# First layer of a two-layer graph network: who issues the zeros, where the first norms are taken, and the order of norm and one-hot

## The chip, the cores and the metric

The kernel runs on one core of one Trainium2 chip. The metric is device time in microseconds for one launch; the time given for a kernel is the median of its runs. All times inside a profile are microseconds from the start of the span, on one profiled execution.

## What is computed

A graph has 12,500 nodes with 256 features each and 200,000 edges (`src`, `dst`, a weight). Cut to what matters:

```
h = relu(layernorm(x))                 # per node, over 256 features
x = x + segment_sum(w[:,None] * (h @ weight)[dst], src)      # layer 0
h = relu(layernorm(x))
x = x + attention over the edges(h) @ Wo.T + bo              # layer 1, 8 heads
```

In layer 0 the edge's message is read at `dst` and summed at `src`. The edges come sorted by `dst`. The change is in layer 0 alone.

## The kernel before, in words

**Layer 0** first builds tables and then runs one long loop. The 200,000 edges are cut into T = 1563 tiles of 128 edges. Since `dst` is sorted, the edges of one tile read few blocks of 128 nodes; each (tile, block) pair is a *row* j, of which there are J = 1660. The loop takes them in NW = 208 windows of W = 8 rows.

For each row, a one-hot of the `dst` within its block (VectorE, `Oh`, line 852) and a weighted matrix that says which edges of the tile have the same `src` (ScalarE, `same`, lines 765 to 776) are multiplied on TensorE (718), copied to SBUF by ScalarE (799) and multiplied with the normed features `h` (734). VectorE adds the product to the tile's slot of `mtw` (`add`, 825) twelve rows behind the window (LAG). A finished tile is added by GpSimd with one indirect DMA of 128 rows into one of four copies of the output in DRAM, `sums[t % 4]` (701). SyncE stands between: it counts finished rows into tiles (`a_tile`), which GpSimd waits for, and landed tiles (`a_landed`), which VectorE waits for before it uses one of 16 slots again.

**The four copies must be zero** before anything is added to them. 72 DMAs write zeros, 704 KB each, 18 for each copy (`zeros`, line 168; `zeroed.per` is 18). All are issued by ScalarE: `sums[0]` and `sums[1]` in the tables' block (36), `sums[2]` and `sums[3]` at the head of the loop's block (36). GpSimd waits for the 18 of `sums[t]` before tile t, for t = 0 to 3 (line 697).

**The norms.** `h` holds all 98 blocks of 128 nodes; they are normed in 14 groups of 7 blocks. Group n needs its rows of `x` (`x_rows`, one DMA of 896 KB, line 162), 7 times two VectorE instructions (836, 838), one square root on ScalarE (442), two small VectorE instructions (434, 436) and 7 ScalarE activations (745). TensorE waits for enough of them (`a_h`).

**The stages.** Every `Block` is a stage: each engine runs its part in the written order, and the next stage begins when all engines have ended. The stages around the change:

- The tables (block with lines 482 to 632). SyncE writes three fields of the edges to DRAM (487 to 491), copies one of them as `srows` (492) and then issues `x_rows` 0 to 2. GpSimd gathers 13 pieces of the fields (508), four in flight; TensorE transposes each (534) and VectorE copies them out (616) with a count (609) before each piece. ScalarE only issues 36 zeros.
- The loop (lines 672 to 887). SyncE issues `x_rows` 3 to 5 and `edge_rows` 0 to 2 (512 KB each, line 669), then begins its counting. ScalarE issues its 36 zeros, then does its part of norms 0 and 1, then `same(0)`, `same(1)`, then the loop over g, two to a window; later `x_rows` and `edge_rows` are issued from there. VectorE does its part of norms 0 and 1, then the windows: in window w norm w + 2 comes first, then `Oh`, then for 8 rows the compare (862) and `add`, then places (868 to 880).

The two sides of a norm wait for each other within one call, on VectorE in `norm_dve`:

```python
e.wait_ge(S(name + "_root"), n)      # ScalarE's square root of this group
e.reciprocal(sc[:, 1, b], sc[:, 0, b]).then_inc(S(name + "_norm"), 1)
```

After layer 0 the engines meet, the four copies are added up, and layer 1 runs; it is the same in both kernels.

Of the kernel before, what the change touches and what calls it, by code (L numbers as in the profile page):

```python
# [7 lines left out]
P = 128  # L8
# [4 lines left out]
NB = 98  # L13
# [9 lines left out]
NS = 4  # L23
ZW = 11 * P
G = 7
# [65 lines left out]
def build(nc, x, src, dst, edge_weight, weight, Wq, bq, Wk, bk, Wv, bv, Wo, bo, out):  # L91
# [17 lines left out]
    with ExitStack() as top:  # L109
# [52 lines left out]
            e.dma_start(h[:, b0:b1, :], x[b0 * P:b1 * P, :].rearrange("(b p) d -> p b d", p=P)).then_inc(  # L162
                xin.sem(g), 16)

        def zeros(e, k):
            part = sums[k].rearrange("(p r) d -> p (r d)", p=P)
            for i in range(zeroed.per):
                e.dma_start(part[:, i * ZW:(i + 1) * ZW], zero[:, :]).then_inc(zeroed.sem(k * zeroed.per + i), 16)

        def edge_loads(e, vec, to, sem):  # L170
            full = 12 * P * P
# [282 lines left out]
        wT = sb(l0a, "wT", [P, JP])  # L454
        sT = sb(l0a, "sT", [P, JP])
        rf = sb(l0a, "rf", [P, 1])
        with ExitStack() as stack:
            NF = 4
            blk = sb(stack, "blk", [P, 13], I32)
            cvec = sb(stack, "cvec", [P, 13])  # L460
            df = sb(stack, "dstf", [P, 13, P])
# [21 lines left out]
            @block.sync  # L483
            def _(e):
                table = fields.rearrange("(c p) f -> p c f", p=P)
                e.wait_ge(edges[2].sem(2), edges[2].value(2))
                e.dma_start(table[:, :, 2 * P:3 * P], wf[:, :, :]).then_inc(rows.sem(0), 16)
                e.wait_ge(S("pr_fields"), 1)
                e.dma_start(table[:, :, P:2 * P], df[:, :, :]).then_inc(rows.sem(1), 16)
                e.wait_ge(S("pr_fields"), 2)  # L490
                e.dma_start(table[:, :, 0:P], sf[:, :, :]).then_inc(rows.sem(2), 16)
                e.dma_start(srows.rearrange("a (c p f) -> p (a c) f", p=P, f=P), sf[:, :, :]).then_inc(put.sem(0), 16)
                for g in range(3):
                    x_rows(e, g)
                e.wait_ge(put.sem(0), put.value(0))

            @block.gpsimd
# [38 lines left out]

            @block.scalar
            def _(e):
                for k in range(NS // 2):
                    zeros(e, k)  # L540

            @block.vector
            def _(e):
                e.wait_ge(edges[1].sem(2), edges[1].value(2))
                e.tensor_scalar(blk[:, :], ints[:, 1, :, 0], 7, None, ALU.logical_shift_right).then_inc(
                    S("pr_blk"), 1)
# [64 lines left out]

                for c in range(13):
                    count(c)
                    for i, to in enumerate((dloc, sT, wT)):
                        e.wait_ge(S("pr_turn"), 3 * c + i + 1)
                        e.tensor_copy(to[:, c * P:(c + 1) * P], psum[3 * (c % 2) + i][:, 0:P]).then_inc(
                            S("pr_column"), 1)
# [22 lines left out]

        with ExitStack() as stack:
            LAG, BACK = 12, 5
            epst = sb(stack, "epst", [P, 1])
            stt = sb(stack, "stt", [P, 4, 6])
            mv = sb(stack, "mv", [P, NB, 2])
            sc = sb(stack, "sc", [P, 3, NB])
            Oh = sb(stack, "Oh0", [P, 2, W, P])
            Sr = ints[:, :, :, :].rearrange("p a b c -> p (a b c)").bitcast(F32)[:, 0:3 * W * P].rearrange(
                "p (s j e) -> p s j e", s=3, j=W)
# [22 lines left out]
            @block.sync  # L672
            def _(e):
                (e_reg[e.engine], *_) = registers(e, "l0s")
                regs = registers(e, "l0t")
                e.sem_inc(S("a_landed"), 1)
                for w in range(3):
                    x_rows(e, w + 3)
                    edge_rows(e, w)
                for t in range(T + BACK):  # L680
                    if t < T:
                        if t % 4 == 0:
                            e.load(regs[:4], lastrow[0:1, t:t + 4])
                            last = [e.snap(r, min_val=1, max_val=J) for r in regs[:4]]

                        e.wait_ge(S("a_row"), last[t % 4])
                        e.sem_inc(S("a_tile"), 1)
                    if t >= BACK:
                        e.wait_ge(sent.sem(t - BACK), sent.value(t - BACK))
                        e.sem_inc(S("a_landed"), 1)  # L690
# [47 lines left out]

            @block.scalar
            def _(e):  # L740
                def norm(n):
                    norm_act(e, "a", n, n + 1, mv, sc, epst)
                    e.wait_ge(S("a_norm"), 2 * n + 2)
                    for b in range(n * G, n * G + G):
                        e.activation(h[:, b, :], h[:, b, :], ACT.Relu, bias=sc[:, 2, b:b + 1],
                                     scale=sc[:, 1, b:b + 1]).then_inc(S("a_h"), 1)

                for k in range(NS // 2, NS):
                    zeros(e, k)
                norm(0)  # L750
                norm(1)
                (e_reg[e.engine], *_) = registers(e, "l0c")
                regs = registers(e, "l0h")

# [27 lines left out]
                for g in range(J // 4):  # L782
                    same(g + 2)
                    v = g // 2
                    if g % 2 == 0:
                        if v + 2 < NG7:
                            norm(v + 2)
                        if v + 6 < NG7:
                            x_rows(e, v + 6)
                        if v + 6 == NG7 - 1:  # L790
                            e.dma_start(h[0:NLAST, NB - 1, :], x[(NB - 1) * P:N, :]).then_inc(hw[24].sem, 16)
                        if v and v + 2 < NW:
                            e.wait_ge(S("a_more"), v * W)
                            e.wait_ge(S("a_off"), v * W)
                            edge_rows(e, v + 2)
# [7 lines left out]
            def _(e):  # L803
# [22 lines left out]
                                           in1=psum[2 + j // 2 % 4][:, j % 2 * D:j % 2 * D + D], op0=ALU.mult,  # L826
                                           op1=ALU.add).then_inc(S("a_row"), 1)

                def norm(n):
                    e.wait_ge(xin.sem(n), xin.value(n))  # L830
                    if n == NG7 - 1:
                        e.wait_ge(hw[24].sem, 16)
                    for b in range(n * G, n * G + G):
                        if b >= 4:
                            e.wait_ge(S("a_stat"), 2 * b - 6)
                        e.bn_stats(stt[:, b % 4, :], h[:, b, :]).then_inc(S("a_stat"), 1)
                        e.wait_ge(S("a_stat"), 2 * b + 1)
                        e.bn_aggr(mv[:, b, :], stt[:, b % 4, :]).then_inc(S("a_stat"), 1)
                    norm_dve(e, "a", n, n + 1, mv, sc)

                e.memset(epst[:, :], 1e-5)
                e.memset(one[:, :], 1.0).then_inc(S("a_one"), 1)
                norm(0)
                norm(1)
                for w in range(NW):
                    j0 = w * W
                    n = min(W, J - j0)
                    if w + 2 < NG7:
                        norm(w + 2)
                    if w >= 2:  # L850
                        e.wait_ge(S("a_weights"), 2 * w - 2)
                    e.tensor_tensor(Oh[:, w % 2, 0:n, :], bcast(iota[:, :], n), rows_of(dloc[:, j0:j0 + n]),  # L852
                                    ALU.is_equal).then_inc(S("a_oh"), 1)
                    e.wait_ge(came.sem(w), came.value(w))
                    for j in range(j0, j0 + n):
                        if j % 4 == 0:
                            e.load(regs[:4], toff[0:1, j:j + 4])
                            row = [e.snap(r, min_val=0, max_val=W - 1) for r in regs[:4]]
# [1149 lines left out]
```

## Time and profile before

| what | us |
|---|---|
| median of 3 runs | 6892.29 (6885.31 to 6894.68) |
| the profiled execution's own time | 6941.69 |
| its span | 6939.9 |
| granted TensorE clock, mean | 0.796 |
| busy: PE / PE loads / DVE / ACT / POOL | 4544.0 / 2978.0 / 4539.5 / 3970.3 / 4648.7 |
| first and last indirect add of layer 0 (line 701) | 233.9 / 3231.6 |

PE is TensorE's matmul, PEld its weight load, DVE VectorE, ACT ScalarE, POOL GpSimd, SPq and ACTq the DMA issues of SyncE and ScalarE. Busy time says how long an engine had an instruction; what an engine waited for stands behind it in brackets (`[idle before <-releaser]`). "issue" is time for which the profile shows no wait. The granted clock is given as a share of 2.4 GHz.

### The profile page before, as it was taken

What the parts mean: (1) busy time and instruction counts of PE and PEld (TensorE: products, weight loads), DVE (VectorE), ACT (ScalarE), POOL (GpSimd) and SP (SyncE); (2) the same over time, 40 slices, a digit from 0 to 9 for tenths busy, and PEclk for the clock granted to TensorE, in tenths of its full rate; (3) what the DMA queues carried; (4) which work ended last, traced back from release to release, by engine and by line L of the source; (5) the groups of instructions that cost most, each with busy time, mean ns of one, the idle gap of its engine ahead of it and who ended that gap; (6) DMA issues with size and microseconds to landing.
All of it is one profiled execution on the core that took longest, in us unless ns stands there. A gap on an engine that the chain in (4) does not pass through costs nothing. (4 is left out here: it accounts for less than half of the span.)

```text
span 6939.9 us, 112013 instructions
## 1 busy us (share of the span) xinstructions
PE 4544.0 (65%) x19717; PEld 2978.0 (43%) x16197; DVE 4539.5 (65%) x12295; ACT 3970.3 (57%) x14482; POOL 4648.7 (67%) x3716
## 2 busy tenths in 40 slices
PE   1356666666666666664886677777777777777777
PEld 1244444444444545553553333334333333434335
DVE  4565555555555666663554777777777777777766
ACT  0665555555555555552332577777777767777761
POOL 1478888888888888887554566666666666666630
PEclk6677777777777777776998888888888888888889
DMA  8767777777777777777874566666666666676756
GB/s 303 196 103 107 106 106 105 104 107 106 108 107 106 106 110 108 109 109 167 274 260 136 173 188 192 192 190 195 194 192 195 200 200 197 201 206 201 204 151 194
DMA packets 644159, 1129.71 MB, mean 163 GB/s; under 512 B 74529, under 2 KB 466795, under 8 KB 643445
## 3 DMA queue, kind: packets, MB, share of 16 engines
q0 software_dynamic: 367600, 678.97, 50.2%
q1 hardware_dynamic: 223985, 273.78, 12.1%
q10 hardware_dynamic: 51860, 169.74, 7.3%
q14 instruction: 546, 4.47, 0.2%
q8 instruction: 168, 2.75, 0.2%
HBM read 929.80 MB, written 451.51 MB: 199 GB/s over the span
## 5 line engine op out<-in xcount | busy, mean ns | idle before, releaser
L701 POOL DMA_INDIRECT sums<-mtw,posIw x1563 | 2492.0, 1594 | 599.5 <-issue 404.5
L1249 POOL DMA_INDIRECT kv<-kvt,sI x1760 | 1774.2, 1008 | 1027.4 <-ACT room L1631 596.1
L1631 ACT ACTIVATE room<-kv,pp 128x33 f32<-128x33 f32 x8800 | 1932.3, 308 | 107.2 <-issue 101.8
L734 PE MATMUL ps<-h,wf 128*128 x3320 | 1220.8, 522 | 310.0 <-DVE mtw L825 237.3
L1551 PE MATMUL ps<-room,Of 128*128 128x264 f32 x3520 | 1130.8, 459 | 372.2 <-DVE acc L1734 189.0
L718 PE MATMUL ps<-Mw,Oh 128*128 128x128 f32 x3320 | 672.6, 368 | 918.6 <-DVE Oh L852 918.6
L825 DVE SCALAR_TENSOR_TENSOR mtw<-mtw,cont,ps 128x256 f32 x1660 | 794.1, 478 | 620.2 <-SPq L690 459.9
L718 PEld LDWEIGHTS ps<-Mw,Oh 128*128 128x128 f32 x3320 | 631.7, 274 | 1035.3 <-DVE Oh L852 1004.4
L734 PEld LDWEIGHTS ps<-h,wf 128*128 128x128 f32 x3320 | 816.9, 263 | 590.1 <-issue 451.4
L1551 PEld LDWEIGHTS ps<-room,Of 128*128 128x128 f32 x3520 | 707.6, 219 | 659.6 <-issue 278.6
L799 ACT COPY wf<-ps 128x512 f32<-128x512 f32 x415 | 242.4, 584 | 1234.4 <-PE ps L718 902.9
L1496 PE MATMUL ps<-qb,OT 128*128 x3520 | 699.3, 301 | 0.0
L1530 PE MATMUL ps<-qb,OT 128*128 x1760 | 534.0, 303 | 244.6 <-DMA qb<-qt 189.0
L862 DVE SCALAR_TENSOR_TENSOR junk<-ints,sT,tri 128x128 f32<-128x128 f32 x1660 | 574.7, 347 | 87.8 <-issue 87.4
L880 DVE TENSOR_TENSOR posIw<-sT,step 128x1 f32 x1660 | 265.1, 160 | 473.1 <-DVE step L870 163.4
L1688 DVE TENSOR_TENSOR room<-ps,kv 128x1024 f32<-128x1024 f32 x440 | 532.1, 1209 | 19.9 <-remote 14.3
L1734 DVE SCALAR_TENSOR_TENSOR acc<-acc,keep,ps 128x264 f32 x880 | 422.3, 480 | 184.2 <-remote 113.4
L765 ACT ACTIVATE off<-ints,sT 128x128 f32 x1660 | 530.1, 390 | 19.9 <-issue 8.6
L776 ACT ACTIVATE Mw<-off,wT 128x128 f32<-128x128 f32 x1660 | 530.0, 390 | 13.4
L1697 DVE TENSOR_REDUCE room<-room 128x32 f32<-128x1024 f32 x440 | 533.7, 1213 | 0.3
L1530 PEld LDWEIGHTS ps<-qb,OT 128*128 128x128 bf16 x1760 | 189.3, 108 | 701.0 <-issue 641.3
L770 ACT ACTIVATE off<-off,one 128x512 f32<-128x512 f32 x415 | 299.4, 721 | 13.5
(224 smaller groups left out, 4796.5 us busy)
## 6 DMA issues: line engine op xcount, KB each, us to landing
qb<-qt SPq DMA_DIRECT2D x880, 192.0 KB
accd<-acc SPq DMA_DIRECT2D x880, 132.0 KB
ints<-srows ACTq DMA_DIRECT2D x205, 512.0 KB
OT<-drows SPq DMA_DIRECT2D x110, 512.0 KB
sums<-zero ACTq DMA_DIRECT2D x72, 704.0 KB
part<-sums SPq DMA_DIRECT2D x56, 896.0 KB
kv<-kvt,sI POOLq DMA_INDIRECT x1760
kvt<-kvo SPq DMA_DIRECT2D x98, 260.0 KB
```

What stands on the lines that cost most here:

```text
L701: e.indirect_dma_start(sums[t % NS], bass.IndirectOffsetOnAxis(ap=posI[:, t % NP:t % NP + 1], axis=0), mt[:, t % NM, :], None, compute_op= ...
L718: m = e.matmul(psum[g % 2][:, j % 4 * P:j % 4 * P + P], lhsT=Oh[:, j // W % 2, j % W, :], rhs=Mw[:, j % 16, :], start=True, stop=True)
L734: m = e.matmul(psum[2 + q % 4][:, j % 2 * D:j % 2 * D + D], lhsT=BT[:, g % 3, j % 4, :], rhs=h[:, bass.ds(own[j % 4], 1), :].rearrange("p ...
L825: e.scalar_tensor_tensor(out=to, in0=to, scalar=cont[:, j:j + 1], in1=psum[2 + j // 2 % 4][:, j % 2 * D:j % 2 * D + D], op0=ALU.mult, op1= ...
L862: e.scalar_tensor_tensor(out=junk[:, j % 4, :], in0=srow, scalar=sT[:, j:j + 1], in1=tri[:, :], op0=ALU.is_equal, op1=ALU.mult, accum_out= ...
L1249: e.indirect_dma_start(kv[:, s % NK, :], None, kvt, bass.IndirectOffsetOnAxis(ap=sI[:, s:s + 1], axis=0)).then_inc(kvs.sem(s), 16)
L1496: return e.add_instruction(mybir.InstMatmult(name=nc.get_next_instruction_name(), engine=e.engine, start_tensor_calc=False, stop_tensor_ca ...
L1530: e.matmul(to, lhsT=hot, rhs=third(j, 0), start=True, stop=False)
L1551: m = e.matmul(psum[6 + j % 2][:, 0:NH * 33], lhsT=Of[:, w % 2, k % W2, :], rhs=pv[:, k % NV, :], start=(k % 2 == 0), stop=(k % 2 == 1))
L1631: e.activation(pv[:, s % NV, h * 33:h * 33 + 33], kv[:, s % NK, D + h * 33:D + h * 33 + 33], ACT.Copy, scale=pp[:, w % 2, h, s % W2:s % W2 ...
L1688: e.tensor_tensor(prod[:, Q % 2, :, :], banks[:, Q % 2 * 2:Q % 2 * 2 + 2, :].rearrange("p b (a d) -> p (b a) d", d=D), kv[:, s:s + 4, 0:D] ...
L1697: e.tensor_reduce(sims[:, w % 2, :, Q % 4 * 4:Q % 4 * 4 + 4].rearrange("p h i -> p i h"), prod[:, Q % 2, :, :].rearrange("p a (h d) -> p a ...
```

## The change

- `zeros` takes a range of the 72 pieces in place of a copy's number. ScalarE issues pieces 0 to 35 and 36 to 55 in the tables' stage. SyncE issues 56 to 71 at the head of the loop's stage, between its rows of edges and of `x`.
- Norms 0 and 1 are taken in the tables' stage: ScalarE between its two runs of zeros, VectorE after its first count. SyncE issues `x_rows` 0 and 1 before the copy to `srows`. The small tiles of the norm move to the outer scope.
- At the head of the loop's stage only norm 2 is taken. In window w, VectorE makes `Oh` first, then takes the statistics of group w + 3, and ends that norm (`norm_dve`) ahead of the window's fifth row. ScalarE ends group v + 2 (`normed0`) and then takes the root of group v + 3.
- `norm` falls apart into `stats0` and `normed0`, which are shown in the diff.

```diff
--- before.py
+++ after.py
@@ -162,10 +162,11 @@
             e.dma_start(h[:, b0:b1, :], x[b0 * P:b1 * P, :].rearrange("(b p) d -> p b d", p=P)).then_inc(
                 xin.sem(g), 16)
 
-        def zeros(e, k):
-            part = sums[k].rearrange("(p r) d -> p (r d)", p=P)
-            for i in range(zeroed.per):
-                e.dma_start(part[:, i * ZW:(i + 1) * ZW], zero[:, :]).then_inc(zeroed.sem(k * zeroed.per + i), 16)
+        def zeros(e, first, end):
+            for i in range(first, end):
+                at = i % zeroed.per * ZW
+                e.dma_start(sums[i // zeroed.per].rearrange("(p r) d -> p (r d)", p=P)[:, at:at + ZW],
+                            zero[:, :]).then_inc(zeroed.sem(i), 16)
 
         def edge_loads(e, vec, to, sem):
             full = 12 * P * P
@@ -454,8 +455,30 @@
         wT = sb(l0a, "wT", [P, JP])
         sT = sb(l0a, "sT", [P, JP])
         rf = sb(l0a, "rf", [P, 1])
+        epst = sb(l0a, "epst", [P, 1])
+        stt = sb(l0a, "stt", [P, 4, 6])
+        mv = sb(l0a, "mv", [P, NB, 2])
+        sc = sb(l0a, "sc", [P, 3, NB])
+
+        def stats0(e, n):
+            e.wait_ge(xin.sem(n), xin.value(n))
+            if n == NG7 - 1:
+                e.wait_ge(hw[24].sem, 16)
+            for b in range(n * G, n * G + G):
+                if b >= 4:
+                    e.wait_ge(S("a_stat"), 2 * b - 6)
+                e.bn_stats(stt[:, b % 4, :], h[:, b, :]).then_inc(S("a_stat"), 1)
+                e.wait_ge(S("a_stat"), 2 * b + 1)
+                e.bn_aggr(mv[:, b, :], stt[:, b % 4, :]).then_inc(S("a_stat"), 1)
+
+        def normed0(e, n):
+            e.wait_ge(S("a_norm"), 2 * n + 2)
+            for b in range(n * G, n * G + G):
+                e.activation(h[:, b, :], h[:, b, :], ACT.Relu, bias=sc[:, 2, b:b + 1],
+                             scale=sc[:, 1, b:b + 1]).then_inc(S("a_h"), 1)
+
         with ExitStack() as stack:
-            NF = 4
+            NF, ZA, ZB = 4, 36, 56
             blk = sb(stack, "blk", [P, 13], I32)
             cvec = sb(stack, "cvec", [P, 13])
             df = sb(stack, "dstf", [P, 13, P])
@@ -489,9 +512,10 @@
                 e.dma_start(table[:, :, P:2 * P], df[:, :, :]).then_inc(rows.sem(1), 16)
                 e.wait_ge(S("pr_fields"), 2)
                 e.dma_start(table[:, :, 0:P], sf[:, :, :]).then_inc(rows.sem(2), 16)
+                x_rows(e, 0)
+                x_rows(e, 1)
                 e.dma_start(srows.rearrange("a (c p f) -> p (a c) f", p=P, f=P), sf[:, :, :]).then_inc(put.sem(0), 16)
-                for g in range(3):
-                    x_rows(e, g)
+                x_rows(e, 2)
                 e.wait_ge(put.sem(0), put.value(0))
 
             @block.gpsimd
@@ -536,11 +560,15 @@
 
             @block.scalar
             def _(e):
-                for k in range(NS // 2):
-                    zeros(e, k)
+                zeros(e, 0, ZA)
+                for n in range(2):
+                    norm_act(e, "a", n, n + 1, mv, sc, epst)
+                    normed0(e, n)
+                zeros(e, ZA, ZB)
 
             @block.vector
             def _(e):
+                e.memset(epst[:, :], 1e-5)
                 e.wait_ge(edges[1].sem(2), edges[1].value(2))
                 e.tensor_scalar(blk[:, :], ints[:, 1, :, 0], 7, None, ALU.logical_shift_right).then_inc(
                     S("pr_blk"), 1)
@@ -611,6 +639,10 @@
 
                 for c in range(13):
                     count(c)
+                    if c == 0:
+                        for n in range(2):
+                            stats0(e, n)
+                            norm_dve(e, "a", n, n + 1, mv, sc)
                     for i, to in enumerate((dloc, sT, wT)):
                         e.wait_ge(S("pr_turn"), 3 * c + i + 1)
                         e.tensor_copy(to[:, c * P:(c + 1) * P], psum[3 * (c % 2) + i][:, 0:P]).then_inc(
@@ -640,10 +672,6 @@
 
         with ExitStack() as stack:
             LAG, BACK = 12, 5
-            epst = sb(stack, "epst", [P, 1])
-            stt = sb(stack, "stt", [P, 4, 6])
-            mv = sb(stack, "mv", [P, NB, 2])
-            sc = sb(stack, "sc", [P, 3, NB])
             Oh = sb(stack, "Oh0", [P, 2, W, P])
             Sr = ints[:, :, :, :].rearrange("p a b c -> p (a b c)").bitcast(F32)[:, 0:3 * W * P].rearrange(
                 "p (s j e) -> p s j e", s=3, j=W)
@@ -674,9 +702,15 @@
                 (e_reg[e.engine], *_) = registers(e, "l0s")
                 regs = registers(e, "l0t")
                 e.sem_inc(S("a_landed"), 1)
-                for w in range(3):
-                    x_rows(e, w + 3)
-                    edge_rows(e, w)
+                edge_rows(e, 0)
+                x_rows(e, 3)
+                zeros(e, ZB, ZB + 5)
+                edge_rows(e, 1)
+                x_rows(e, 4)
+                zeros(e, ZB + 5, ZB + 10)
+                edge_rows(e, 2)
+                x_rows(e, 5)
+                zeros(e, ZB + 10, NS * zeroed.per)
                 for t in range(T + BACK):
                     if t < T:
                         if t % 4 == 0:
@@ -738,17 +772,8 @@
 
             @block.scalar
             def _(e):
-                def norm(n):
-                    norm_act(e, "a", n, n + 1, mv, sc, epst)
-                    e.wait_ge(S("a_norm"), 2 * n + 2)
-                    for b in range(n * G, n * G + G):
-                        e.activation(h[:, b, :], h[:, b, :], ACT.Relu, bias=sc[:, 2, b:b + 1],
-                                     scale=sc[:, 1, b:b + 1]).then_inc(S("a_h"), 1)
-
-                for k in range(NS // 2, NS):
-                    zeros(e, k)
-                norm(0)
-                norm(1)
+                norm_act(e, "a", 2, 3, mv, sc, epst)
+                normed0(e, 2)
                 (e_reg[e.engine], *_) = registers(e, "l0c")
                 regs = registers(e, "l0h")
 
@@ -783,8 +808,10 @@
                     same(g + 2)
                     v = g // 2
                     if g % 2 == 0:
-                        if v + 2 < NG7:
-                            norm(v + 2)
+                        if 3 <= v + 2 < NG7:
+                            normed0(e, v + 2)
+                        if v + 3 < NG7:
+                            norm_act(e, "a", v + 3, v + 4, mv, sc, epst)
                         if v + 6 < NG7:
                             x_rows(e, v + 6)
                         if v + 6 == NG7 - 1:
@@ -826,33 +853,22 @@
                                            in1=psum[2 + j // 2 % 4][:, j % 2 * D:j % 2 * D + D], op0=ALU.mult,
                                            op1=ALU.add).then_inc(S("a_row"), 1)
 
-                def norm(n):
-                    e.wait_ge(xin.sem(n), xin.value(n))
-                    if n == NG7 - 1:
-                        e.wait_ge(hw[24].sem, 16)
-                    for b in range(n * G, n * G + G):
-                        if b >= 4:
-                            e.wait_ge(S("a_stat"), 2 * b - 6)
-                        e.bn_stats(stt[:, b % 4, :], h[:, b, :]).then_inc(S("a_stat"), 1)
-                        e.wait_ge(S("a_stat"), 2 * b + 1)
-                        e.bn_aggr(mv[:, b, :], stt[:, b % 4, :]).then_inc(S("a_stat"), 1)
-                    norm_dve(e, "a", n, n + 1, mv, sc)
-
-                e.memset(epst[:, :], 1e-5)
                 e.memset(one[:, :], 1.0).then_inc(S("a_one"), 1)
-                norm(0)
-                norm(1)
+                stats0(e, 2)
+                norm_dve(e, "a", 2, 3, mv, sc)
                 for w in range(NW):
                     j0 = w * W
                     n = min(W, J - j0)
-                    if w + 2 < NG7:
-                        norm(w + 2)
                     if w >= 2:
                         e.wait_ge(S("a_weights"), 2 * w - 2)
                     e.tensor_tensor(Oh[:, w % 2, 0:n, :], bcast(iota[:, :], n), rows_of(dloc[:, j0:j0 + n]),
                                     ALU.is_equal).then_inc(S("a_oh"), 1)
+                    if w + 3 < NG7:
+                        stats0(e, w + 3)
                     e.wait_ge(came.sem(w), came.value(w))
                     for j in range(j0, j0 + n):
+                        if j == j0 + 4 and w + 3 < NG7:
+                            norm_dve(e, "a", w + 3, w + 4, mv, sc)
                         if j % 4 == 0:
                             e.load(regs[:4], toff[0:1, j:j + 4])
                             row = [e.snap(r, min_val=0, max_val=W - 1) for r in regs[:4]]
```

## Rows read from the trace of the kernel before

**Rows 1.** The page, part 1: busy time of the engines.

```profile
PE 4544.0 (65%) x19717; PEld 2978.0 (43%) x16197; DVE 4539.5 (65%) x12295; ACT 3970.3 (57%) x14482; POOL 4648.7 (67%) x3716
```

**Rows 2.** Line 701 alone, whole span and 500 to 1000 us: ns min/median/max, first and last start.

```profile
L701 POOL DMA_INDIRECT sums<-mtw,posIw x1563: 1557/1558/2547, 233.9 to 3231.6; - x196
...
L701 POOL DMA_INDIRECT sums<-mtw,posIw x265: 1558/1558/2051, 498.9 to 998.8; - x133
```

**Rows 3.** Waits, 138 to 300 us: us in total, times, longest.

```profile
POOL sums L701 <- SPq L687: 106.9, 10, 92.2
DVE sc L434 <- ACT sc L442: 68.9, 8, 56.8
```

**Rows 4.** Timeline of the issuing queues: start, us.

```profile
65.04 23.41 SPq L492 DMA_DIRECT2D srows<-srcf  x1
...
85.64 1.72 ACTq L168 DMA_DIRECT2D sums<-zero  x1
...
138.15 59.05 ACTq L168 DMA_DIRECT2D sums<-zero  x36
```

**Rows 5.** Timeline of the tables' stage.

```profile
106.46 1.11 POOL L508 DMA_INDIRECT fg<-fields,pair_t  x1 [71.59 <-DMA fields<-srcf]
...
115.00 0.29 DVE L616 COPY dloc<-ps 128x128 f32<-128x128 f32 x1 [25.83 <-PE ps L534]
```

**Rows 6.** Stretches: us, busy of the engines, PE clock, DMA share, GB/s.

```profile
106.00:115.00 9.00, 0.48 (x3) 0.50 (x3) 0.00 (x0) 0.00 (x0) 3.96 (x4) 0.50 1.00 318
115.00:138.00 23.00, 10.11 (x38) 6.28 (x36) 22.75 (x71) 0.00 (x0) 8.51 (x9) 0.50 0.42 128
...
180.00:197.00 17.00, 0.00 (x0) 0.00 (x0) 0.00 (x0) 0.00 (x0) 0.00 (x0) 0.50 1.02 424
...
211.00:213.00 2.00, 0.00 (x0) 0.00 (x0) 0.00 (x0) 1.94 (x6) 0.00 (x0) 0.50 0.75 310
```

**Rows 7.** Timeline of norm 0 in the loop's stage.

```profile
138.25 0.43 DVE L836 BATCH_NORM_STATS2 stt<-h 128x6 f32<-128x256 f32 x1
...
141.88 0.18 DVE L838 BATCH_NORM_AGGREGATE mv<-stt 128x2 f32<-128x6 f32 x1
...
197.24 1.28 ACT L442 ACT_TABLE_LOAD   x1 [197.24 <-issue]
...
199.10 0.17 DVE L436 SCALAR_TENSOR_TENSOR sc<-mv,sc 128x7 f32<-128x7 f32 x1
...
199.30 3.55 ACT L745 ACTIVATE h<-h,sc 128x256 f32<-128x256 f32 x7 [0.47 <-DVE sc L436]
```

**Rows 8.** Timeline of DVE: the one-hots of windows 0 to 3 and 11 to 13.

```profile
217.61 1.22 DVE L852 TENSOR_TENSOR Oh<-iota,dloc 128x1024 f32<-128x1024 f32 x1
229.24 1.22 DVE L852 TENSOR_TENSOR Oh<-iota,dloc 128x1024 f32<-128x1024 f32 x1
244.19 1.22 DVE L852 TENSOR_TENSOR Oh<-iota,dloc 128x1024 f32<-128x1024 f32 x1
262.30 1.22 DVE L852 TENSOR_TENSOR Oh<-iota,dloc 128x1024 f32<-128x1024 f32 x1
...
403.65 1.22 DVE L852 TENSOR_TENSOR Oh<-iota,dloc 128x1024 f32<-128x1024 f32 x1
416.57 1.22 DVE L852 TENSOR_TENSOR Oh<-iota,dloc 128x1024 f32<-128x1024 f32 x1
429.60 1.22 DVE L852 TENSOR_TENSOR Oh<-iota,dloc 128x1024 f32<-128x1024 f32 x1
```

**Rows 9.** Timeline of POOL: its first indirect add, and the last it was late for.

```profile
233.86 1.65 POOL L701 DMA_INDIRECT sums<-mtw,posIw  x1 [92.19 <-SPq L687]
...
406.62 1.56 POOL L701 DMA_INDIRECT sums<-mtw,posIw  x1 [2.79 <-SPq L687]
```

**Rows 10.** Waits, 262.3 to 333.2 us (four windows).

```profile
DVE mtw L825 <- PE ps L734: 4.1, 3, 1.4
...
DVE sc L434 <- ACT sc L442: 1.5, 4, 0.4
```

## The prediction

> **What bounds the kernel now.** By busy time no engine stands out; POOL leads with 67% [rows 1]. So I went to layer 0's loop and asked POOL's own line first. Its 1563 indirect adds run from 233.9 to 3231.6 us, and between 500 and 1000 us 264 of them start within 499.9 us, 1.89 us apart: 1.56 busy and a fixed gap, with no stall [rows 2]. So POOL is the bound of layer 0 from some tile on, nothing before it matters but when that regime begins, and a saving at the start is not taken back later. POOL's last late tile is at 406.62 [rows 9]. It is tile 76: window 11 starts at 403.65 [rows 8], its first row is 88, and `add` runs 12 rows behind (here a row is a tile, since the first tiles all lie in one block of nodes). The question is when tile 76 comes after the change.
>
> **Why it is late now.** POOL waits 92.2 us for its first tile [rows 3, 9]. Behind that is VectorE, which ends the statistics of norm 0 at 142.1 and then waits 56.8 us for ScalarE's root [rows 3, 7], since ScalarE is still issuing 36 pieces of zeros, 59.05 us at 1.64 us each [rows 4]. That pace is the DMAs': share 1.02, 424 GB/s, so a piece of 0.72 MB takes 1.70 us [rows 6]. The zeros are all written at 212.5 (211 plus 310/424 of 2 us) [rows 6], but ScalarE was free at 197.2 and the first product came at 234. The DMAs had room between the stages: share 0.42 and 128 GB/s from 115 to 138 us [rows 6]. From window 3 to window 11 each window has a norm and takes 17.7 us (141.35 over 8), while windows without one take 13.0 [rows 8] and eight tiles cost POOL 15.1. So in these windows VectorE sets the pace, and after them POOL.
>
> **The change, part by part.**
>
> *Rows of x ahead of `srows`.* The third field lands at 106.46 [rows 5]. From 106 to 115 the DMAs moved 2.86 MB [rows 6], which was `srows` (0.85), the first rows of x (0.92) and four gathers (0.79). With `srows` behind, x group 0 lands near 110 and group 1 near 113.5. SyncE's issue of `srows` (23.4 us, a full queue) only moves [rows 4]; its landing is hidden, as the loop's first reader is over 30 us later. What x group 2 loses is hidden in the same way.
>
> *Norms 0 and 1 in the tables.* Statistics of a group take 3.81 us, root to last small instruction 2.03 with the table load (1.28) and 0.75 without [rows 7]. VectorE: 110 + 3.8 + 2.0 = 115.8, + 3.8 + 0.75 = 120.4. It now starts copying the gathered pieces at 115.00 [rows 5], so its part of the tables ends 5.4 us later, at 143.6 instead of 138.15. ScalarE is done with norm 1 at 120.4 + 3.55 = 124 [rows 7].
>
> *20 pieces from ScalarE there.* They start at 124; before, zeros started again at 138.15. How many pieces a queue holds: ScalarE's issue ended 15.3 us before the zeros did, which is 6.5 MB or 9 pieces. So 11 pieces are waited for: 11 × 1.70 = 18.7, plus 7 gathers of 0.2 MB in between, 3.3, gives 146. That, not VectorE, ends the stage: the loop's stage begins 8 us later than before.
>
> *16 pieces from SyncE.* Before, 36 pieces, three groups of x and three `edge_rows` (30.3 MB) took 138.15 to 212.5, 408 GB/s with the ramp. After, the same 30.3 MB plus 1.4 of gathers and 2.3 of later loads that ScalarE issues meanwhile start at 124: 34.0 / 0.408 = 83.4 us, so the last piece lands near 207.5. Tile 3 needs it. Six pieces stand behind x group 5, which so lands near 196. Behind the blocked SyncE waits the first tile's count (`a_tile`); SyncE is through about 15 us before the last landing, thus ahead of tile 3.
>
> The Trainium skill (DMA: Bandwidth & Descriptors, Rules for kernel authors) speaks against this part: spreading DMAs over several issuers gives no bandwidth, since all run on the same 16 engines. My rows agree with a shared total, and by that rule alone, were the zeros' end what tile 0 waits for today, the change would bring only the few us by which they end sooner (first "no change" rival below).
>
> *The first windows.* The stage begins at 146 with 9 pieces queued; `edge_rows` 0 and x group 3 share the DMAs with them (7.9 MB, 18.7 us) and land by 165. Window 0 then needs 11.63 less its one-hot of 1.22 [rows 8]: 175. x group 4 lands near 179 (five pieces 8.5, `edge_rows` 1.2, itself 2.2, ScalarE's group 6 2.2); window 1 from there 14.95 - 1.22 = 13.7: 193. x group 5 at 196; window 2 from there 18.1 - 1.2 = 16.9 [rows 8]: window 3 starts at **212.9 instead of 262.30, 49.4 us earlier**.
>
> *One-hots ahead of the norms, root not waited for.* Removed per window: the 0.4 us wait for the root (1.5 in four) and, of the 1.0 us wait for products (4.1 in four), some [rows 10], since TensorE gets its one-hot earlier. The statistics themselves (3.8) stay on VectorE. ScalarE now waits for them behind `normed0`, and its copies stand behind that wait; VectorE reads those products one window later, so I cost it at nothing; uncovered, it would be the same 4 us as now. Bounds of the saving: 0 and 1.4 per window; I take 0.7 (the root's whole wait, a third of the other, as the old order delays its one-hots by most of the norm), 5.6 over eight windows.
>
> *The sum.* Window 10 starts at 212.9 + (141.35 - 5.6) × 7/8 = 331.7. Its first row now comes after one-hot, statistics and the 1.75 us that rows 8 and 9 show (406.62 - 403.65 - 1.22): tile 68 at 338.5. Eight tiles at 1.89 later tile 76 starts: **353.6 instead of 406.62, 53 us earlier**. With no saving it is 48, with the full one 58. POOL's own line from tile 3 gives 207.5 + 73 × 1.886 = 345.2, 61 earlier, the cap. Everything after tile 76 is unchanged. The profiled execution takes 6941.7, so 6888.7 after; it stands 49.4 above the median, and I take the same gain off both: 6892.3 - 53 = **6839 us**.
>
> **Rivals.**
> *POOL never starves (gain 58 to 70).* If the queue holds fewer pieces or x lands sooner, window 3 starts earlier; the cap of 61 moves only with the zeros' end, 1 us for 1 us. For it: my serial sum over x groups 3 to 5 is pessimistic, since each transfer is charged alone. Against: a normed window must then take under 15.1, and the statistics alone add 3.8 to 13.0. About 6829. Chance 0.18.
> *The start is slower (gain 20 to 45).* The gathers share saturated DMAs from 124 on; the first took from 106.46 to 114.5 in a saturated stretch. If six pieces come late by 2 us each and SyncE's loads of x behind zeros slip by as much, window 3 starts at 230: gain about 33, 6859. Against: gathers run four deep. Chance 0.20.
> *No change.* Tile 0 would be held by the zeros themselves, the rule's case: gain at most 212.5 - 207.5 = 5, 6887. Against: 21 us lie between the zeros' end and tile 0 today, and 57 us of VectorE's wait are for ScalarE. The same result comes if the two norms' rows land so late that ScalarE's zeros again end near 197. Chance 0.05.
> *Slower.* One mechanism: the steady pace. `epst`, `stt`, `mv` and `sc` move to the outer scope, so the loop's tiles lie elsewhere, and every tile of POOL costs its pace 1487 more times after tile 76. If the pace of 1.886 us rises by 36 ns (2%), the gain of 53 is gone; at 60 ns it is 89 - 53 = 36 us slower, 6928. For: the mean is already above the median of 1.558 + 0.30, so something adds now and then. Against: instructions and operands of the steady loop are the same. Chance 0.05.
> The forecast's own case has 0.52 (6833 to 6845).
>
> **How the numbers follow.** About 0.2%, 14 us, can be told from no change. Faster: 0.52 + 0.18 + 0.20 = 0.90; same 0.05; slower 0.05. The range runs from a gain of 72 (the cap of 61 with zeros ending 10 us sooner) to one of 26 (most of the slow start): 6820 to 6866.
>
> **What would show it.** Right: VectorE's first statistics near 110, a second run of zeros at 124, no 57 us wait for the root; the loop's stage from 146; zeros' end near 207; one-hots of window 3 near 213 and of window 11 near 349, windows between them about 17; POOL's last late tile near 354 and its end near 3179; every stage after that as before. Wrong: a stage of the tables that ends after 155, windows 3 to 10 above 17.7 us (the new order costs), POOL stalls after 400 us, or a pace off 1.89.

## The result, and the profile after

The changed kernel takes 6870.63 us in the median of 9 runs (6849.30 to 6875.02), the kernel before beside it 6890.89: ratio 0.9966, 95% interval 0.9955 to 0.9978. It is 20 us faster, where 53 were forecast; 6870.6 lies outside the range of 6820 to 6866. The profiled execution spans 6868.8 us, 71 less than the one before, but of that only 24 lie in layer 0; the rest is layer 1, which is the same in both kernels and differs by itself from one execution to the next (in the profiles of the runs below it spans 3113 to 3145 us). So from here on I compare positions inside layer 0.

POOL's line (first and last start), and the timeline of DVE's one-hots of windows 0 to 3 and 11 and 12:

```profile
L735 POOL DMA_INDIRECT sums<-mtw,posIw x1563: 1557/1559/2588, 200.9 to 3207.5; - x196
```

```profile
150.64 1.22 DVE L864 TENSOR_TENSOR Oh<-iota,dloc 128x1024 f32<-128x1024 f32 x1
...
185.48 1.22 DVE L864 TENSOR_TENSOR Oh<-iota,dloc 128x1024 f32<-128x1024 f32 x1
...
206.44 1.22 DVE L864 TENSOR_TENSOR Oh<-iota,dloc 128x1024 f32<-128x1024 f32 x1
...
225.67 1.22 DVE L864 TENSOR_TENSOR Oh<-iota,dloc 128x1024 f32<-128x1024 f32 x1
...
378.89 1.21 DVE L864 TENSOR_TENSOR Oh<-iota,dloc 128x1024 f32<-128x1024 f32 x1
392.22 1.22 DVE L864 TENSOR_TENSOR Oh<-iota,dloc 128x1024 f32<-128x1024 f32 x1
```

Against [rows 2] the last add comes at 3207.5 instead of 3231.6. Against [rows 8] two things are to be seen. Window 3 starts at 225.7, 36.6 us earlier than before, where 49.4 were forecast. And from there to window 11 it takes 153.2 us, not 141.35: **19.15 us a window, 1.5 more than before**, where 0.7 less were forecast. POOL's last late tile, with the time that it stood idle:

```profile
367.60 1.56 POOL L735 DMA_INDIRECT sums<-mtw,posIw  x1 [3.61 <-SPq L721]
```

The stages themselves went as forecast. Timeline of the tables' stage and the head of the loop's:

```profile
109.55 0.43 DVE L470 BATCH_NORM_STATS2 stt<-h 128x6 f32<-128x256 f32 x1 [21.80 <-DMA h<-in_x]
...
118.68 0.82 ACTq L168 DMA_DIRECT2D sums<-zero  x2
...
146.01 3.51 POOL L728 MEMSET mtw<- 128x4096 f32 x1 [12.14 <-POOLq L480]
...
163.65 0.43 DVE L470 BATCH_NORM_STATS2 stt<-h 128x6 f32<-128x256 f32 x1 [11.79 <-DMA h<-in_x]
...
175.84 1.28 ACT L790 ACTIVATE off<-ints,sT 128x128 f32 x4 [13.46 <-DMA ints<-srows]
...
179.41 0.20 DVE L435 RECIPROCAL sc<-sc 128x7 f32<-128x7 f32 x1 [9.61 <-ACT sc L443]
```

First statistics at 109.6 (forecast 110), zeros again at 118.7 (124), the loop's stage from 146.0 (146), x group 3 at 163.7 (165). That the stage begins as forecast is in part luck: the 20 pieces were issued from 118.7 to 144.6, which is 26 us where 22 were reckoned, and they began 5 us earlier than reckoned. The last two lines are what I did not foresee: ScalarE stands 13.5 us for the rows of edges of window 1, and VectorE 9.6 us behind it. The waits of 138 to 300 us, which answer to [rows 3]:

```profile
POOL sums L735 <- SPq L721: 79.0, 19, 51.4
...
ACT off L790 <- DMA ints<-srows: 26.9, 4, 13.5
...
DVE sc L435 <- ACT sc L443: 13.8, 3, 9.6
```

The 57 us for the root have gone, as forecast, and 27 us of waits for rows of edges have come.

### The profile page after: what moved, and what is told of

Same layout as the page of the kernel before. It is cut to its first block and busy times, and to the rows that moved or that the text cites. A ratio compares the mean times of both kernels' runs of the same rounds, so it can differ in the third digit from the quotient of the medians.

```text
span 6868.8 us, 112013 instructions
## 1 busy us (share of the span) xinstructions
PE 4547.2 (66%) x19717; PEld 2990.5 (44%) x16197; DVE 4538.6 (66%) x12295; ACT 3955.8 (58%) x14482; POOL 4666.2 (68%) x3716
## 5 line engine op out<-in xcount | busy, mean ns | idle before, releaser
L1265 POOL DMA_INDIRECT kv<-kvt,sI x1760 | 1797.1, 1021 | 965.0 <-ACT room L1647 580.3
L896 DVE TENSOR_TENSOR posIw<-sT,step 128x1 f32 x1660 | 265.4, 160 | 476.9 <-DVE step L886 163.7
L790 ACT ACTIVATE off<-ints,sT 128x128 f32 x1660 | 530.2, 390 | 44.4 <-DMA ints<-srows 26.9
L801 ACT ACTIVATE Mw<-off,wT 128x128 f32<-128x128 f32 x1660 | 530.0, 390 | 13.4
L795 ACT ACTIVATE off<-off,one 128x512 f32<-128x512 f32 x415 | 299.4, 722 | 13.5
```

The lines of the kernel that those rows point to most:

```text
L1265: e.indirect_dma_start(kv[:, s % NK, :], None, kvt, bass.IndirectOffsetOnAxis(ap=sI[:, s:s + 1], axis=0)).then_inc(kvs.sem(s), 16)
```

## The experiments

The runs below were made on three chips, one for e1 to e4, one for e5 to e8 and one for e9 to e11; which chip the first nine were on is not known. On the three the kernel before takes 6342 to 6352 us, but layer 0 has the same times to a few us. The table has each run's ratio to the kernel before on the same chip, the start of window 3, the mean of windows 3 to 10, the start of tile 76 on POOL and POOL's last add.

| run | ratio (95%) | window 3 | us a window | tile 76 | last add |
|---|---|---|---|---|---|
| before, first profile | | 262.3 | 17.67 | 406.6 | 3231.6 |
| changed, first profile | 0.9966 (0.9955 to 0.9978) | 225.7 | 19.15 | 382.5 | 3207.5 |
| e10_changed_again | 0.9965 (0.9955 to 0.9976) | 227.6 | 19.21 | 384.8 | 3212.9 |
| e1_edges_first | 0.9961 (0.9949 to 0.9972) | 222.7 | 19.02 | 378.4 | 3198.9 |
| e2_old_window | 0.9950 (0.9933 to 0.9966) | 229.5 | 17.65 | 373.7 | 3195.2 |
| e3_order_alone | 1.0018 (1.0007 to 1.0029) | 254.9 | 19.01 | 411.8 | 3234.3 |
| e4_loads_ahead | 0.9939 (0.9923 to 0.9956) | 224.0 | 17.36 | 367.7 | 3189.2 |
| e9_end_at_top | 0.9948 (0.9929 to 0.9968) | 217.2 | 18.21 | 367.7 | 3194.0 |
| e5_norm_top | 0.9921 (0.9903 to 0.9938) | 221.4 | 17.2 (16.74) | 360.1 | 3182.9 |
| e6_rows_first | 0.9934 (0.9914 to 0.9953) | 210.8 | 18.72 | 364.1 | 3186.8 |
| e7_rows_and_loads | 0.9923 (0.9904 to 0.9942) | 209.0 | 17.15 | 358.5 | 3184.3 |
| e8_rows_and_top | 0.9936 (0.9918 to 0.9955) | 213.5 | 17.1 (16.67) | 359.1 | 3181.8 |
| e11_rows_old_window | 0.9929 (0.9907 to 0.9951) | 211.1 | 17.56 | 358.2 | 3181.1 |

From tile 76 to the last add it takes 2825.0 us in both first profiles, and 2820.5 to 2828.2 in all: a last add is good to some 4 us either way, and differences below that are read at tile 76. Many ratios overlap as well (e2's with e10's, for one); there the traces decide.

In e5 and e8 the statistics stand ahead of the one-hot, so only seven of the eight stretches hold a norm, and a window with one takes (133.88 - 13.4)/7 = 17.2 (mean of all eight in brackets). For the same reason their window 3 is counted 3.8 us later than in the other runs.

### Is it the window's order? e2_old_window, e3_order_alone

```diff
# e2: the changed kernel, VectorE's window as before
+                    if 3 <= w + 2 < NG7:
+                        stats0(e, w + 2)
+                        norm_dve(e, "a", w + 2, w + 3, mv, sc)
                     (one-hot)
-                    if w + 3 < NG7:
-                        stats0(e, w + 3)
...
-                        if j == j0 + 4 and w + 3 < NG7:
-                            norm_dve(e, "a", w + 3, w + 4, mv, sc)
# e3: the reverse edit on the kernel before
```

ScalarE's root goes with it in both.

> The changed kernel with the loop in the old order: in window w statistics and the end of norm w + 2, then the one-hot; ScalarE root and activations together. Start and zeros as changed. If the new order is what costs in windows 3 to 10, they take 17.7 us again instead of 19.15, window 11 comes 141 us after window 3 instead of 153, and layer 0 ends up to 12 us earlier than in the changed kernel. If the longer windows come from elsewhere (the traffic of the zeros, the tiles' new places), they stay at 19.15.

> The kernel before with the new order in the loop alone (three norms at the head of the loop, one-hot first, statistics of group w + 3, norm ended before the fifth row). Zeros and tables as before. If the order costs by itself, windows 3 to 10 take 19.15 us instead of 17.7 and the last late tile of POOL comes some 10 us after 406.6, the kernel 0.15% slower than before. If the order gains as the prediction had it, they take 17.0 and the last late tile comes near 401.

One-hots of windows 3 and 11, first of e2, then of e3:

```profile
229.48 1.22 DVE L866 TENSOR_TENSOR Oh<-iota,dloc 128x1024 f32<-128x1024 f32 x1
...
370.71 1.22 DVE L866 TENSOR_TENSOR Oh<-iota,dloc 128x1024 f32<-128x1024 f32 x1
```

```profile
254.86 1.22 DVE L855 TENSOR_TENSOR Oh<-iota,dloc 128x1024 f32<-128x1024 f32 x1
...
406.95 1.22 DVE L855 TENSOR_TENSOR Oh<-iota,dloc 128x1024 f32<-128x1024 f32 x1
```

141.2 us with the old order, 152.1 with the new one (153.2 in the changed kernel), whatever the zeros do. The order costs 1.4 to 1.5 us a window, 12 us over the eight; at tile 76, where POOL takes over, 9 are left of them (373.7 against 382.5). Alone it makes the kernel before slower, 1.0018. In e3 tile 76 came 5 us later and the last add 2.7, not the 10 expected: its window 3 started 7 us earlier than in the profile of before. Part of that is that profile itself. Its third field landed at 106.46 [rows 5], where it came at 99.1 in e3 and between 97.0 and 102.9 in the others, and its loop's stage began at 138.2, in e3 at 131.9. So the base of the forecast's sum is some 6 us late against e3, as far as one profile of each can tell.

### Why does the order cost? e4_loads_ahead, e9_end_at_top, e5_norm_top

Window 5 in the changed kernel, DVE's timeline, the compares and adds that come after a gap, and then the same of the kernel before:

```profile
269.57 0.35 DVE L878 SCALAR_TENSOR_TENSOR junk<-ints,sT,tri 128x128 f32<-128x128 f32 x1 [0.52 <-issue]
...
271.46 0.48 DVE L852 SCALAR_TENSOR_TENSOR mtw<-mtw,cont,ps 128x256 f32 x1 [1.40 <-issue]
...
275.36 0.35 DVE L878 SCALAR_TENSOR_TENSOR junk<-ints,sT,tri 128x128 f32<-128x128 f32 x1 [1.05 <-issue]
...
277.12 0.48 DVE L852 SCALAR_TENSOR_TENSOR mtw<-mtw,cont,ps 128x256 f32 x1 [1.41 <-PE ps L768]
```

```profile
300.12 0.48 DVE L825 SCALAR_TENSOR_TENSOR mtw<-mtw,cont,ps 128x256 f32 x1 [0.97 <-issue]
...
303.06 0.35 DVE L862 SCALAR_TENSOR_TENSOR junk<-ints,sT,tri 128x128 f32<-128x128 f32 x1 [0.39 <-issue]
...
304.86 0.48 DVE L825 SCALAR_TENSOR_TENSOR mtw<-mtw,cont,ps 128x256 f32 x1 [1.44 <-PE ps L734]
```

The gaps stand where registers are loaded: every fourth row takes its place in `Sr` (`toff`) and its slot (`mrow`, `frow`) from SBUF. After the statistics the first compare is 0.52 late and the first add 1.40 instead of 0.97; in the middle of the window, behind the norm's end, it is 1.05 instead of 0.39. The gap that is named as a wait for PE is as long as before. Together 0.52 + 0.43 + 0.66 = 1.6 more, less the 0.4 of the root saved: 1.2 of the 1.5 us a window. A gap before the places is 0.2 longer in this window (0.71 against 0.52); the rest I have not placed.

e4 moves the loads only. Those of the rows and of the slots now also stand together, once before the statistics and once before the norm's end (guards cut out):

```diff
                    (one-hot)
+                    row = rows_at(j0); slots_of(j0 - LAG)
                     stats0(e, w + 3)
...
                         if j == j0 + 4:
+                            row = rows_at(j); slots_of(j - LAG)
                             norm_dve(e, "a", w + 3, w + 4, mv, sc)
```

> The changed kernel with VectorE's register loads of a normed window moved: those of the first four rows ahead of the statistics (behind the one-hot), those of the next four ahead of the end of the norm. Theory register loads: in the new order they stand behind steps that wait for one another and run uncovered, 0.5 + 0.4 us after the statistics and 0.65 after the norm's end; then the windows fall from 19.15 to between 17.6 and 18.3. Rival, ScalarE: it waits for the statistics before its copy, so products come late and VectorE waits for them; then the windows stay at 19.15 here.

19.15 became 17.36, a little better than the 17.6 to 18.3 expected. DVE's waits of 224 to 310 us in that run (five windows):

```profile
DVE sc L435 <- issue: 7.4, 5, 1.6
...
DVE stt L470 <- issue: 3.1, 5, 0.7
...
DVE mtw L860 <- issue: 0.3, 1, 0.3
```

The loads are not free in their new place: 0.6 stand before the statistics and 1.5 before the norm's end, 2.1 in a window. But the gaps before the adds, 1.40 and 1.41, have gone, the one named for PE too, though nothing was changed on ScalarE or TensorE. So that one had been loads as well, or at least covered by them, and the rival falls. The four gaps of window 5 were 4.4 us, and 2.0 in their place gives 2.4 less; that window became 2.3 us shorter.

e9 takes apart the two places, e5 covers both:

```diff
# e9
                     n = min(W, J - j0)
+                    if 3 <= w + 2 < NG7:
+                        norm_dve(e, "a", w + 2, w + 3, mv, sc)
                     (one-hot, then stats0(e, w + 3))
-                        if j == j0 + 4 and w + 3 < NG7:
-                            norm_dve(e, "a", w + 3, w + 4, mv, sc)
# e5: as e9, and stats0(e, w + 3) ahead of the one-hot
```

> The changed kernel with one thing moved: the end of norm w + 2 stands at the top of window w in place of the end of norm w + 3 before the fifth row of window w. One-hot and statistics as changed. By the theory of register loads this takes away the uncovered loads in the middle of the window and leaves those behind the statistics: windows of 18.3 to 18.6, between 19.15 and the 17.2 that both moves gave. If all of the cost lay in the middle: 17.5 or less; if none: 19.1.

> The changed kernel with another order on VectorE: in window w the end of norm w + 2 (its root is long ready), then the statistics of group w + 3, then the one-hot; ScalarE as changed. The one-hot stands behind the statistics again and covers the register loads of the first rows; nothing stands in the middle of the window. Theory register loads: 17.2 to 17.6 us a window (the old order's 17.65 less the 0.4 us wait for the root), as in the run with the loads moved. Rival: a late one-hot makes products late, which is what the new order was to mend; then 18 or more.

e9: 18.21, so 0.94 for the norm's end in the middle of the window (expected 18.3 to 18.6). e5: 17.2, so another 1.0 for the statistics between one-hot and rows (expected 17.2 to 17.6). That the one-hot's 1.2 us cover the loads behind it, and a step that waits for the one before it does not, is how I read these; shown is that the place of the loads and of the chained steps is what costs.

The table shows one thing more, at the start. ScalarE stands as long for rows of edges in e9 as in the changed kernel (28.2 us against 26.9, up to 225 us), and yet window 3 starts at 217.2, 8.5 us earlier. DVE's timeline of e9, to be held against the 9.61 above:

```profile
180.44 0.20 DVE L435 RECIPROCAL sc<-sc 128x7 f32<-128x7 f32 x1 [3.21 <-ACT sc L443]
180.76 1.22 DVE L866 TENSOR_TENSOR Oh<-iota,dloc 128x1024 f32<-128x1024 f32 x1
```

With the norm's end in the middle of window 0, VectorE stands for a root that ScalarE takes only behind the late rows, and has four rows of its window still to do after it. At the top of window 1 the same root comes at nearly the same time (180.4), and those rows are done. So the new order also passed ScalarE's wait on to VectorE.

### The slow start: e1_edges_first, e6_rows_first

`same(2)` is the first call in ScalarE's loop, at g = 0: it needs the rows of edges of window 1 before window 0's products. They stand behind x group 3 and five zeros in SyncE's queue. The order in SyncE's queue, in short:

```
changed  edge_rows 0, x 3, 5 zeros, edge_rows 1, x 4, 5 zeros, edge_rows 2, x 5, 6 zeros
e1       edge_rows 0, 1, 2, x 3, 5 zeros, x 4, 5 zeros, x 5, 6 zeros
e6       edge_rows 0, x 3, edge_rows 1, x 4, edge_rows 2, x 5, 16 zeros
e6 also, on ScalarE: edge_rows(v + 2) ahead of x_rows(v + 6)
```

> SyncE issues the three rows of edges of windows 0 to 2 first, then x group 3, 5 zeros, x group 4, 5 zeros, x group 5, 6 zeros. Theory FIFO: ScalarE's same(2), the first call of the loop over g, needs the edge rows of window 1, which stand behind 5 zeros and x group 3 in SyncE's queue; that is its 13.5 us wait at 175.8, and VectorE's norm 3 waits 9.6 us for the root behind it. Then here both waits vanish, window 1 starts near 176 instead of 185.5, window 3 near 215 instead of 225.7, and layer 0 ends about 10 us earlier than in the changed kernel. Rival, rows of x: the start is held by x groups 4 and 5; then window 2 stays near 206 and window 3 near 226.

> The changed kernel, window order untouched, with SyncE's rows of edges 0 to 2 and of x 3 to 5 all ahead of its 16 zeros, and on ScalarE the rows of edges of window v + 2 issued ahead of x group v + 6. Theory FIFO: a short transfer behind a long one in its own queue waits for both (14.2 us in the run with edges first, where the rows of window 3 stood behind x group 7; 13.5 in the changed kernel). Then no wait of ScalarE for rows of edges is over 6 us, window 1 starts near 178, window 3 near 211, and the windows after it stay at 19.1. Rival, shared engines: any transfer among the zeros takes about 14 us whatever stands before it; then ScalarE still waits 6 to 14 us and window 3 stays at 222 or later.

e1 is half a miss: window 1 starts at 180.0 instead of 185.5 (176 was expected; x group 3 came 3.3 us later, behind all three rows of edges), but window 3 at 222.7, 3 us earlier instead of 10. The wait moved to the next rows of edges. The rival that x groups 4 and 5 hold the start falls: VectorE waits 1.0 us for group 4 here, and for neither in the changed kernel. ACT's timeline of e1:

```profile
186.10 0.39 ACTq L162 DMA_DIRECT2D h<-in_x  x1
187.07 0.37 ACTq L697 DMA_DIRECT2D ints<-srows  x1
...
206.63 1.28 ACT L789 ACTIVATE off<-ints,sT 128x128 f32 x4 [14.21 <-DMA ints<-srows]
```

ScalarE itself issues x group 7 (0.92 MB in 896 rows of 1 KB) and behind it, in the same queue, the rows of window 3 (0.5 MB); these are there 19.6 us later. In e6 the rows stand ahead of x in both queues. ScalarE's waits of 138 to 300 us in that run, and then POOL's tile 3:

```profile
ACT off L785 <- DMA ints<-srows: 8.6, 4, 2.7
```

```profile
210.67 1.56 POOL L730 DMA_INDIRECT sums<-mtw,posIw  x1 [17.87 <-DMA sums<-zero]
```

The rows of window 3 in e6, from their issue to the end of ScalarE's wait for them:

```profile
181.61 0.37 ACTq L697 DMA_DIRECT2D ints<-srows  x1
...
189.41 1.28 ACT L785 ACTIVATE off<-ints,sT 128x128 f32 x4 [2.37 <-DMA ints<-srows]
```

No wait for rows of edges is over 2.7 us, and window 3 starts at 210.8; the windows behind it took 18.72, not the 19.1 expected. The same rows took 19.6 us behind x group 7 and 7.8 ahead of it, both times while zeros were written, so the rival, that anything among the zeros takes 14 us, falls for them. The rows of window 1 did take 15.4 us in e6 as well (issued at 150.3, used at 165.7, behind x group 3); what took their wait away is that they were issued 11 us earlier. So how long a short transfer takes goes by what stands before it in its own queue, and when it is needed by where it stands in the issuer's list. The Trainium skill (DMA: Bandwidth & Descriptors, Queues, rings and completion order) has each DMA engine take turns between the queues and go through each in order. The trace agrees: 19.6 us for 0.5 MB behind 0.9 MB among zeros, 7.8 us ahead of it. And now POOL stands 17.9 us for the last zeros, at tile 3. e6 changes both queues at once; what each brings was not tried.

### Both together: e7_rows_and_loads, e8_rows_and_top, e11_rows_old_window

> Rows first and register loads ahead together. If the two causes add up: window 3 near 211, windows of 17.36, window 11 near 350 instead of 378.9, layer 0 ending 29 us earlier than in the changed kernel, thus 50 us or more before the kernel before: the prediction's 53. If POOL's first tiles are held by the last zeros (near 207) the end stays some us behind that.

> Rows first with the end of the norm at the window's top and the statistics ahead of the one-hot. As the run before it within 3 us, if both ways cover the register loads alike.

> Rows first with the old window order. Window 3 between 211 and 216, windows of 17.65, layer 0 ending near 3186: if it does, the new window order is not needed for any of the gain, and what it was to bring (the root not waited for) is worth 3 us at most.

The three end layer 0 at 3184.3, 3181.8 and 3181.1, 47 to 50 us before the first profile of the kernel before, and e7's window 11 starts at 346.3. In device time they are 40 to 48 us faster than the kernel before on their chips; the forecast's 53 are not reached. The two remedies do not add up: covered loads without rows first (e5) bring tile 76 to 360.1, rows first with the new order (e6) to 364.1, both together (e7) to 358.5. In e7 and e8 too POOL waits 17.8 and 18.2 us at tile 3 for the last zeros, then is late five or six times more by 0.8 to 3.0 us, the last near 294, and by more than its fixed 0.3 us gap never after. e11 says most: with the *old* window order and the rows first, tile 76 comes at the same time within 1 us and the end within 3. The new order is not needed for any of the gain. Which of the other parts brings it, the norms in the tables' stage or the zeros shared with SyncE, no run takes apart.

e10 is the changed kernel again:

> The changed kernel itself, beside the others and on the same chip as they. The ends of layer 0 say 12 us more than the run with the old window order and 24 us more than those with rows first and covered loads; so its ratio to the kernel before should be near 0.9965, as first measured, and its windows 19.15.

0.9965 and 19.21 us a window, as on the first chip.

## Why the prediction was wrong

Right: POOL sets layer 0's pace from some tile on, and a gain at the start is kept to the end (its last late tile is now tile 68 at 367.6; tile 76 follows at 382.5, 24 us earlier than at 406.62, and the last add is 24 us earlier too). From there on both take 2825.0 us, so the rival of a slower steady pace falls. The stage of the tables, the second run of zeros, the stage's start and x group 3 came within 1 to 5 us, the stage's start by two misses that cancel. The end of the zeros fits: tile 3 starts at 206.6 (forecast 207.5) without a wait, so they had ended by then; where tile 3 does wait for them (e1, e5 to e9, e11) it starts at 208.5 to 211.0. The rule that the prediction took from the Trainium skill (DMA: Bandwidth & Descriptors, Rules for kernel authors), by which several issuers bring no bandwidth, was weighed rightly for the old kernel, whose wait was for ScalarE's issuing: tile 0 came 33 us earlier (233.9 to 200.9) though the zeros ended only some 6 us sooner (212.5, and by 206.6). In e6 to e8 the shared DMAs are what tile 3 waits for.

Tile 76 came at 382.5 instead of 353.6. Of these 29 us window 3 holds 13, the seven windows behind it 15 and the head of window 10 the last 1.3, so two terms of the sum hold all:

1. *"Window 0 then needs 11.63 less its one-hot: 175"* failed. I gave each transfer to the window whose number it has. ScalarE works one window ahead of VectorE, so `edge_rows` 1 is needed in window 0, `edge_rows` 2 in window 1. ScalarE had them at 175.8 and 189.6. Window 3 came at 225.7 instead of 212.9: **13 us**. With the rows first (e6) it is 210.8. That this is near 212.9 is in part luck: the sum let windows 1 and 2 wait for x groups 4 and 5, 4 and 3 us, and neither kernel waits for them, while its windows 1 and 2 took 16.1 and 18.6 us instead of 14.95 and 18.1. The text charged SyncE's zeros to x groups and to POOL, never to the rows of edges that stood in the same list. Nor did it see that the new order makes VectorE share that wait: with the norm's end at the window's top (e9) 8.5 of the 13 us are gone with the rows as late as ever.
2. *"I cost it at nothing"* and *"I take 0.7"* a window failed. Measured is 1.5 more a window instead of 0.7 less: **15 us** over the seven windows of the sum, and 1.3 at the head of the next. I bounded the saving by two waits of [rows 10] and took zero as the lower bound, with no reason that excluded a loss. The reason against was in the trace: gaps called "issue" before the rows where registers are loaded, 0.97 and 0.39, which grew to 1.40 and 1.05 when chained steps stood in front of them. The gain that I looked for, products in time, was not there: the wait named for PE went when the loads alone were moved. Only the root's 0.4 us was saved.

By the medians 33 us are missing (53 less 20), not 29. The other 4 may be the late start of the profile of before, from which the sum was reckoned; that is not shown.

The range failed by the same steps: its slow case held late x rows, but no window above 17.7, though I had named that as what would make me wrong.

## What to carry to other kernels

A cost of zero for an instruction that is moved needs its cover named on both sides: what it covered where it stood, and what stands behind it where it goes. Here a one-hot of 1.2 us covered register loads, and steps that wait for one another did not. An instruction that waits for another engine is best put where the rest of its own engine's window no longer stands behind it. When bulk transfers are moved to another queue, list for every small transfer behind them which engine reads it first, not which loop index it carries, and put the small ones ahead.

## What the runs showed that I had not expected

Layer 1 is some 525 us shorter in the later runs (3134 us in e10, 3138 in e2, against 3661) with the same program. The stretch 3600 to 5000 us, first in the changed kernel's first profile, then in e2's (us, busy of the engines, granted clock, DMA share, GB/s):

```profile
3600.00:5000.00 1400.00, 1010.43 (x5048) 554.84 (x3518) 1035.93 (x1736) 916.92 (x4125) 867.30 (x880) 0.84 0.64 187
```

```profile
3600.00:5000.00 1400.00, 1144.70 (x6146) 609.82 (x4248) 1258.27 (x2112) 1125.95 (x5133) 1040.37 (x1072) 0.94 0.76 228
```

The granted clock is 0.84 on the one and 0.94 on the other, and every engine gets through 21 to 24% more instructions in the same time. Both are means between TensorE's two levels, 1.2 and 2.4 GHz. Layer 0, which POOL bounds, has the same times on both to a few us, and the change brings the same 20 us (6352.2 to 6332.3 in e10). Whether it is the chip, and whether the clock is the cause or goes along with something else, was not tried.
